# One exponential, one cast and one subtraction of 2048 columns per head in place of two halves

## The chip, the cores and the metric

The kernel runs on one core of one Trainium2 chip. The metric is the device time of one execution, in microseconds. TensorE does the matmuls, ScalarE the activations (ACT in the rows), VectorE the elementwise work (DVE), GpSimd small operations and scattered stores (POOL), and SyncE (SP) issues most transfers.

## What is computed

A decoder layer over x of 4 x 512 tokens of 512 values. Of the three parts only the attention matters here:

```
q = layernorm(x) @ Wq        # 16 heads of 128
k, v = layernorm(x) @ Wkv    # one key and value head, shared by all 16
sim  = (4 * l2norm(q)) @ (4 * l2norm(k)).T
attn = softmax(sim)
out  = layernorm((attn @ v) @ Wout)
x = x + out
```

Then every token goes through one of four gated experts chosen by its id, and then through a feed-forward with weights of three values. All is in fp32 in the reference.

## The kernel before, in words

**Precision.** fp32 products are made of 16-bit ones: a number is split into a high part (a cast) and a low part (the number less its high part), and three matmuls take high x high, high x low and low x high (split_products, lines 252 to 254).

**Heads as steps.** The attention is a loop of 64 steps (STEPS), one per batch and head; step g is head g % 16 of batch g // 16. A step has 512 queries by 512 keys: scores is [keys, queries] in four PSUM banks, S, 2048 columns of fp32 on 128 partitions. ScalarE takes the exponential of S into P32 in SBUF (exponentials). VectorE casts P32 to bf16 (ph) and subtracts (pl), in probabilities. TensorE multiplies both with V (values); the sum of the probabilities is a column of ones beside V. ph and pl are double buffered, P32 and S are not.

**What TensorE does in step g**, in this order: scores(g), values(g - 1), in six steps of the 64 keys_values (the projection for the next batch), from step 16 on outputs(g - 16), a quarter of the output projection of one tile, and up to step 57 queries(g + 6), the query projection of four heads for one tile of 128 tokens. The order is written out by hand in each engine's program, and semaphores tie the engines together.

**The query bank.** queries(u) writes one PSUM bank, QB. ScalarE takes squares (query_squares, line 834), GpSimd a reciprocal root (query_norm), ScalarE writes the high part (query_high, 843) and VectorE the low part (query_low, line 1171), both straight from the bank. For u under 20 the bank alternates between QB and OUTB, and queries(u) waits for query_low(u - 2); from u = 21 all use QB, and queries(u) waits for query_low(u - 1):

```
                elif u >= 20:
                    pe.wait_ge(q_lo, u if u > 20 else 19)
```

**What ScalarE does in step g:** query_squares(g + 5), exponentials of both halves, query_high(g + 5), for some steps a cast of inputs, head_high(g - 1) in two pairs (line 862: the head's result scaled by the reciprocal of its sum), then small pieces of other work: query weights in steps 1 to 4, copies and squares of keys and values, sums and rounding of the feed-forward's weights.

**What VectorE does in step g:** probabilities of half 0, head_sums(g - 1, 0) (a reciprocal, line 1188), query_low(g + 5), head_sums(g - 1, 1), probabilities of half 1, head_low(g - 1) (line 1194), then normalization of inputs and of finished rows, and rounding.

**Semaphores around the change:** s_ps counts halves of scores, p_exp halves of exponentials, p_lo halves of subtractions. scores(g) waits half by half until the exponential of step g - 1 has read S; exponentials(g) wait half by half until the subtraction of step g - 1 has read P32; values(g) waits for both halves of p_lo and for head_low(g - 1), which has read O.

Of the kernel before, what the change touches and what calls it, by code (L numbers as in the profile page):

```python
# [13 lines left out]
ALU = mybir.AluOpType  # L14
ACT = mybir.ActivationFunctionType
# [4 lines left out]
HEADS, DH = 16, 128  # L20
# [3 lines left out]
STEPS = B * HEADS  # L24
# [14 lines left out]
def decoder_layer(nc, x, ids, ctx_w, g_norm, Wq, Wkv, Wout, g_out, w1, w2, out):  # L39
# [8 lines left out]
    with stack:  # L48
# [175 lines left out]
        def ph(g):  # L224
            return P16[:, (g % 2) * 4096:(g % 2) * 4096 + 2048].bitcast(BF16)

        def pl(g):
            return P16[:, (g % 2) * 4096 + 2048:(g % 2) * 4096 + 4096]
# [307 lines left out]
        def _(pe):  # L536
            def keys_values(n):
                b, j = divmod(n, 2)
                bank = kvbank(n)
                for i in range(2):  # L540
                    t = 2 * j + i
                    pe.wait_ge(xt[t], 16 * (b + 1))
                    if n == 0:
                        pe.wait_ge(wkv_lo, 1)
                    if n >= 2 and i == 0:
                        pe.wait_ge(p_exp, 2 * (HEADS * (b - 1) + 11 + j) + 1)
                    for c in range(DC):
                        lh = [XT[b % 2][:, (s * DC + c) * N + t * P:(s * DC + c) * N + (t + 1) * P]
                              for s in range(2)]
                        rh = [WKV[:, (s * DC + c) * 256:(s * DC + c + 1) * 256] for s in range(2)]  # L550
                        last = split_products(bank[:, i * 256:(i + 1) * 256], lh[0], lh[1], rh[0], rh[1],
                                              c == 0, c == DC - 1)
                last.then_inc(kv_ps, 1)
# [19 lines left out]
            def scores(g):  # L573
                b, h = divmod(g, HEADS)
                grp, hh = divmod(g, 4)
                if h == 0:
                    pe.wait_ge(kt, 16 * (b + 1))
                if hh == 0:
                    for t in range(NT):
                        pe.wait_ge(qt[t], 16 * (grp + 1))  # L580
                for half in range(2):
                    if g == 0:
                        pe.wait_ge(q_lo, 4)
                    else:
                        pe.wait_ge(p_exp, 2 * (g - 1) + half + 1)
                    if half == 0 and kv_at(g - 1) is not None:
                        pe.wait_ge(kv_f, kv_at(g - 1) - 1)
                    for j in (2 * half, 2 * half + 1):
                        last = split_products(
                            S[:, j * 512:(j + 1) * 512], KT[:, b % 2, j * P:(j + 1) * P],  # L590
                            KT[:, b % 2, N + j * P:N + (j + 1) * P], QT[grp % 2][:, hh * N:(hh + 1) * N],
                            QT[grp % 2][:, (4 + hh) * N:(5 + hh) * N], True, True)
                    last.then_inc(s_ps, 1)

            def values(g):
                b = g // HEADS
                pe.wait_ge(p_lo, 2 * g + 2)
                if g % HEADS == 0:
                    pe.wait_ge(v_lo, 2 * b + 2)
                if g == 0:  # L600
                    pe.wait_ge(k_lo, 2)
                for t in range(NT):
                    if t % 2 == 0 and g >= 1:
                        pe.wait_ge(o_lo, 2 * (g - 1) + t // 2 + 1)
                    o = o_half(t // 2)[:, t % 2, :]
                    for j in range(NT):
                        a = j * N + t * P
                        nc.tensor.matmul(o, ph(g)[:, a:a + P], V[:, b % 2, j, 0:129], start=j == 0,  # L608
                                         stop=False)
                        nc.tensor.matmul(o[:, 0:128], ph(g)[:, a:a + P], V[:, b % 2, j, 130:258],  # L610
                                         start=False, stop=False)
                        last = nc.tensor.matmul(o, pl(g)[:, a:a + P], V[:, b % 2, j, 0:129], start=False,  # L612
                                                stop=j == NT - 1)
                    if t % 2:
                        last.then_inc(o_ps, 1)

            def outputs(n):
                b, s = divmod(n, HEADS)
                t, q = divmod(s, 4)
                k = b * NT + t  # L620
                if n == 0:
                    pe.wait_ge(q_lo, 20)
                if t == 0 and b == 0:
                    pe.wait_ge(wo_lo, 4 * (q + 1))
                if q == 0:
                    if k == 4:
                        pe.wait_ge(w_set, 1)
                    if 1 <= k <= 12:
                        pe.wait_ge(out_cp, k)
                    elif k > 12:  # L630
                        pe.wait_ge(p_exp, 2 * STEPS)
                for i in range(4):
                    h = 4 * q + i
                    if t == 0:
                        pe.wait_ge(ot[i], (b * 4 + q + 1) * 16)
                        if b == 3:
                            pe.wait_ge(ot_l[i], (q + 1) * 16)
                    lh = [OT[:, ot_block(b, h, s_, t) * P:(ot_block(b, h, s_, t) + 1) * P] for s_ in range(2)]
                    w = h * 2 * D
                    last = split_products(outbank(k), lh[0], lh[1], WOA[:, w:w + D], WOA[:, w + D:w + 2 * D],  # L640
                                          h == 0, h == HEADS - 1)
                last.then_inc(out_c, 1)
# [131 lines left out]
        def _(act):  # L774
# [69 lines left out]
                                                ACT.Copy, scale=rn[:, u % 2, i:i + 1])  # L844
                last.then_inc(q_hi, 1)

            def exponentials(g, half):
                act.wait_ge(s_ps, 2 * g + half + 1)
                if g >= 1:
                    act.wait_ge(p_lo, 2 * (g - 1) + half + 1)  # L850
                nc.scalar.activation(P32[:, half * 1024:(half + 1) * 1024], S[:, half * 1024:(half + 1) * 1024],  # L851
                                     ACT.Exp, bias=off_p).then_inc(p_exp, 1)

            def head_high(g):
                if g >= 2:
# [91 lines left out]
            for g in range(STEPS):  # L947
                b, h = divmod(g, HEADS)
                if out_at(g, 0) is not None:
                    out_copy(out_at(g, 0))  # L950
                if g >= 1 and g + 5 < STEPS:
                    query_squares(g + 5)
                for half in range(2):
                    exponentials(g, half)
                if g >= 1 and g + 5 < STEPS:
                    query_high(g + 5)
                if prep_at(g, 3) is not None:
                    input_high(prep_at(g, 3))
                if out_at(g, 3) is not None:
                    h_high(out_at(g, 3))  # L960
                if g >= 1:
                    head_high(g - 1)
                if kv_at(g) is not None:
                    kv_copy(kv_at(g))
                if kv_at(g) is not None:
                    key_squares(kv_at(g))
                    value_high(kv_at(g))
                if kv_at(g - 1) is not None:
                    key_high(kv_at(g - 1))
                if 1 <= g < 1 + DC:  # L970
                    query_weight(3, g - 1)
                for p in piece_at(g):
                    weight_sum(p)
                if b == 1:
                    ctx_high(h)
                if g >= 2 * HEADS + 3:
                    tern_low(g - 2 * HEADS - 3)
                if g >= 2 * HEADS + 1:
                    tern_scale(g - 2 * HEADS - 1)
# [84 lines left out]
        def _(dve):  # L1064
# [108 lines left out]
                        rn[:, u % 2, i:i + 1], qtok(u)[:, i * P:(i + 1) * P], ALU.mult, ALU.subtract)  # L1173
                last.then_inc(q_lo, 1)

            def probabilities(g, half):
                dve.wait_ge(p_exp, 2 * g + half + 1)
                if g >= 2:
                    dve.wait_ge(o_ps, 2 * (g - 1))
                cols = slice(half * 1024, (half + 1) * 1024)  # L1180
                nc.vector.tensor_copy(ph(g)[:, cols], P32[:, cols]).then_inc(p_hi, 1)  # L1181
                dve.wait_ge(p_hi, 2 * g + half + 1)
                nc.vector.tensor_tensor(pl(g)[:, cols], P32[:, cols], ph(g)[:, cols], ALU.subtract  # L1183
                                        ).then_inc(p_lo, 1)

            def head_sums(g, bank):
                dve.wait_ge(o_ps, 2 * g + bank + 1)
# [117 lines left out]
            for g in range(STEPS):  # L1305
# [2 lines left out]
                    ctx_low(g - 1 - HEADS)  # L1308
                if kv_at(g - 2) is not None:
                    key_low(kv_at(g - 2))  # L1310
                probabilities(g, 0)
                if g == 2 * HEADS:
                    weight_scales_set()
                if g >= 1:
# [2 lines left out]
                    query_low(g + 5)  # L1317
                if g >= 1:
                    head_sums(g - 1, 1)
                probabilities(g, 1)  # L1320
                if g >= 1:
                    head_low(g - 1, 0)
                    head_low(g - 1, 1)
# [325 lines left out]
```

## Time and profile before

| | us |
|---|---|
| median of 3 runs | 966.65 |
| the runs | 963.07, 966.65, 969.02 |
| profiled execution, its own time | 969.39 |
| its span | 967.7 |
| TensorE busy | 920.4 (95%) |
| VectorE busy | 698.8 (72%) |
| ScalarE busy | 616.8 (64%) |
| GpSimd busy | 324.8 (34%) |

The 64 steps fill the span from about 40 to 680 us, the rest is the experts and the feed-forward. Busy shares are means over the span and say nothing of order: an engine with time to spare can still be late where another waits for it. The trace gives each instruction's start and length, and for an idle time ahead of one what ended it. A matmul of 512 columns is shown with 0.38 us, but the next one starts 0.216 us after it, since they are pipelined; so stretches of TensorE are measured from start to start.

### The profile page before, as it was taken

To read this page: it belongs to the slowest core of one execution; us is meant where nothing else is said; L and a number is where in the kernel's file an instruction comes from. 1 tells how busy PE (TensorE), PEld (TensorE's weight loads), DVE (VectorE), ACT (ScalarE), POOL (GpSimd) and SP (SyncE) were. 2 spreads that over 40 slices of the span, in tenths; PEclk is the share of its full clock that TensorE was granted. 3 is DMA by queue.
4 is the path that set the end of the run, shared out by engine and by line. 5 is a ranking of instruction groups with operands and counts; after the bars stand their busy time and mean duration, and the time that the engine had idled before them with its cause. 6 is when DMAs were issued, how large, how long until landed. Compare 5 with 4: busy or idle time off the path is not lost.

```text
span 967.7 us, 19126 instructions
## 1 busy us (share of the span) xinstructions
PE 920.4 (95%) x6577; PEld 520.8 (54%) x6592; DVE 698.8 (72%) x1535; ACT 616.8 (64%) x1571; POOL 324.8 (34%) x450
## 2 busy tenths in 40 slices
PE   5999999999999999999999999999896999999994
PEld 3466676555656566556665565566442444444441
DVE  6799977687786768778677667778262478877782
ACT  4877767667777666667666676665201269988472
POOL 3578866113332323334231322221141012322221
PEclk9999999999999999999999999999997999999999
DMA  9647557567776553564444444349976988544253
GB/s 244 170 89 143 111 109 130 137 165 180 207 169 159 135 127 99 120 143 115 100 99 121 99 115 109 95 120 173 205 183 140 182 191 162 128 99 97 63 131 87
DMA packets 305663, 131.86 MB, mean 136 GB/s; under 512 B 275296, under 2 KB 279904, under 8 KB 305568
## 3 DMA queue, kind: packets, MB, share of 16 engines
q1 hardware_dynamic: 301648, 117.77, 55.3%
q0 software_dynamic: 3920, 12.86, 4.0%
q8 instruction: 54, 0.88, 0.4%
q14 instruction: 41, 0.34, 0.1%
HBM read 42.76 MB, written 20.99 MB: 66 GB/s over the span
## 4 chain that ended last, share of the span: by engine, by line
PE 79%; DVE 5%; issue 3%; ACT 3%; DMA 3%; SPq 2%; POOL 1%; DVEq 0%; ACTq 0%; POOLq 0%
PE S L252 7%; PE S L254 7%; PE S L253 7%; PE O L610 6%; PE O L608 5%; PE QB L252 5%; PE QB L254 5%; PE QB L253 5%; PE O L612 5%; PE OUTB L252 5%; PE OUTB L253 5%; PE OUTB L254 5%; PE S L732 3%; PE OUTB L750 3%; PE O L702 2%
## 5 line engine op out<-in xcount | busy, mean ns | idle before, releaser
L608 PE MATMUL O<-V,P 128*128 128x129 f16 x1024 | 179.0, 219 | 1.3 <-DVE P L1183 1.2
L610 PE MATMUL O<-V,P 128*128 128x128 f16 x1024 | 179.1, 221 | 0.0
L612 PE MATMUL O<-V,P 128*128 128x129 f16 x1024 | 178.9, 218 | 0.0
L1181 DVE CAST P<-P 128x1024 bf16<-128x1024 f32 x128 | 93.9, 733 | 114.8 <-ACT P L851 114.7
L1183 DVE TENSOR_TENSOR P<-P 128x1024 f16<-128x1024 f32 x128 | 160.7, 1255 | 4.4
L851 ACT ACTIVATE P<-S,cst 128x1024 f32<-128x1024 f32 x128 | 142.5, 1116 | 27.2 <-PE S L254 25.4
L1517 POOL TENSOR_SCALAR qst<-qs 128x4 f32<-128x4 f32 x64 | 14.7, 229 | 351.8 <-ACT junk L834 351.8
L834 ACT ACTIVATE junk<-QB 128x128 bf16<-128x128 f32 x208 | 54.8, 278 | 102.8 <-PE QB L254 102.8
L862 ACT ACTIVATE OTOK<-O,rd 128x128 f16<-128x128 f32 x256 | 80.8, 376 | 40.8 <-DVE rd L1188 40.3
L608 PEld LDWEIGHTS O<-V,P 128*128 128x128 bf16 x1024 | 98.5, 96 | 9.5 <-DVE P L1183 2.3
L610 PEld LDWEIGHTS O<-V,P 128*128 128x128 bf16 x1024 | 99.2, 97 | 7.2
L612 PEld LDWEIGHTS O<-V,P 128*128 128x128 f16 x1024 | 100.8, 98 | 0.0
L252 PE MATMUL S<-XQA,KT 128*128 128x512 f16 x256 | 97.2, 380 | 0.3 <-DMA XQA<-P 0.3
L253 PE MATMUL S<-XQA,KT 128*128 128x512 f16 x256 | 97.0, 379 | 0.0
L254 PE MATMUL S<-XQA,KT 128*128 128x512 f16 x256 | 97.0, 379 | 0.0
L252 PE MATMUL OUTB<-WOA,OTA 128*128 128x512 f16 x208 | 79.5, 382 | 2.4 <-ACT OS L873 2.4
L252 PE MATMUL QB<-WQA,XQA 128*128 128x512 f16 x208 | 79.3, 381 | 2.5 <-DVE QTOKR L1171 2.5
L254 PE MATMUL QB<-WQA,XQA 128*128 128x512 f16 x208 | 79.6, 383 | 0.0
L253 PE MATMUL QB<-WQA,XQA 128*128 128x512 f16 x208 | 79.4, 382 | 0.0
L253 PE MATMUL OUTB<-WOA,OTA 128*128 128x512 f16 x208 | 79.4, 382 | 0.0
L254 PE MATMUL OUTB<-WOA,OTA 128*128 128x512 f16 x208 | 79.3, 381 | 0.0
L1518 POOL TENSOR_TENSOR rn<-qst,half 128x4 f32<-128x4 f32 x64 | 71.8, 1123 | 5.4
(238 smaller groups left out, 1952.2 us busy)
## 6 DMA issues: line engine op xcount, KB each, us to landing
SIDE<-in_L_ffn_w_dram SPq DMA_DIRECT2D x64, 256.0 KB, 3.2
OTA<-sorted_rows SPq DMA_DIRECT2D x4, 1028.0 KB, 6.5
OTA<-in_L_attn_Wq_dram SPq DMA_DIRECT2D x4, 1024.0 KB, 7.5
SIDE<-in_L_attn_Wout_dram SPq DMA_DIRECT2D x16, 256.0 KB, 3.1
SIDE<-in_ctx_dram SPq DMA_DIRECT2D x16, 256.0 KB
ctx_split<-SIDE SPq DMA_DIRECT2D x16, 256.0 KB, 3.7
ROWB<-in_x_dram SPq DMA_DIRECT2D x16, 256.0 KB, 3.3
w_tern<-SIDE SPq DMA_DIRECT2D x32, 128.0 KB, 3.0
```

Of the source, the lines that this page charges most:

```text
L252: nc.tensor.matmul(o, lh, rh, start=first, stop=False)
L253: nc.tensor.matmul(o, lh, rl, start=False, stop=False)
L254: return nc.tensor.matmul(o, ll, rh, start=False, stop=last)
L608: nc.tensor.matmul(o, ph(g)[:, a:a + P], V[:, b % 2, j, 0:129], start=j == 0, stop=False)
L610: nc.tensor.matmul(o[:, 0:128], ph(g)[:, a:a + P], V[:, b % 2, j, 130:258], start=False, stop=False)
L612: last = nc.tensor.matmul(o, pl(g)[:, a:a + P], V[:, b % 2, j, 0:129], start=False, stop=j == NT - 1)
L834: last = nc.scalar.activation(junk[:, i * P:(i + 1) * P], qbank(u)[:, i * P:(i + 1) * P], ACT.Square, scale=16.0 / WS, accum_out=qs[:, u % ...
L851: nc.scalar.activation(P32[:, half * 1024:(half + 1) * 1024], S[:, half * 1024:(half + 1) * 1024], ACT.Exp, bias=off_p).then_inc(p_exp, 1)
L862: last = nc.scalar.activation(OTOK[:, g % 2, t * P:(t + 1) * P], o_tile(t), ACT.Copy, scale=rd[:, g % 2, t:t + 1])
L1181: nc.vector.tensor_copy(ph(g)[:, cols], P32[:, cols]).then_inc(p_hi, 1)
L1183: nc.vector.tensor_tensor(pl(g)[:, cols], P32[:, cols], ph(g)[:, cols], ALU.subtract).then_inc(p_lo, 1)
L1518: nc.gpsimd.tensor_tensor(rn[:, s, :], qst[:, s, :], half4[:, :], ALU.pow).then_inc(q_rn, 1)
```

## The change

The exponential, the cast and the subtraction of a step each become one instruction over 2048 columns. p_exp and p_lo count steps rather than halves, and all waits on them are recounted. scores(g) waits for the whole exponential of step g - 1 before either half.

```diff
@@ scores and values, TensorE
-                        pe.wait_ge(p_exp, 2 * (g - 1) + half + 1)
+                        pe.wait_ge(p_exp, g)
...
-                pe.wait_ge(p_lo, 2 * g + 2)
+                pe.wait_ge(p_lo, g + 1)
@@ ScalarE
-            def exponentials(g, half):
-                act.wait_ge(s_ps, 2 * g + half + 1)
+            def exponentials(g):
+                act.wait_ge(s_ps, 2 * g + 2)
                 if g >= 1:
-                    act.wait_ge(p_lo, 2 * (g - 1) + half + 1)
-                nc.scalar.activation(P32[:, half * 1024:(half + 1) * 1024], S[:, half * 1024:(half + 1) * 1024],
-                                     ACT.Exp, bias=off_p).then_inc(p_exp, 1)
+                    act.wait_ge(p_lo, g)
+                nc.scalar.activation(P32[:, :], S[:, :], ACT.Exp, bias=off_p).then_inc(p_exp, 1)
@@ VectorE
-            def probabilities(g, half):
-                dve.wait_ge(p_exp, 2 * g + half + 1)
+            def probabilities(g):
+                dve.wait_ge(p_exp, g + 1)
                 if g >= 2:
                     dve.wait_ge(o_ps, 2 * (g - 1))
-                cols = slice(half * 1024, (half + 1) * 1024)
-                nc.vector.tensor_copy(ph(g)[:, cols], P32[:, cols]).then_inc(p_hi, 1)
-                dve.wait_ge(p_hi, 2 * g + half + 1)
-                nc.vector.tensor_tensor(pl(g)[:, cols], P32[:, cols], ph(g)[:, cols], ALU.subtract
-                                        ).then_inc(p_lo, 1)
+                nc.vector.tensor_copy(ph(g), P32[:, :]).then_inc(p_hi, 1)
+                dve.wait_ge(p_hi, g + 1)
+                nc.vector.tensor_tensor(pl(g), P32[:, :], ph(g), ALU.subtract).then_inc(p_lo, 1)
@@ the loop over steps, VectorE
-                probabilities(g, 0)
+                probabilities(g)
                 if g == 2 * HEADS:
                     weight_scales_set()
                 if g >= 1:
@@
                     query_low(g + 5)
                 if g >= 1:
                     head_sums(g - 1, 1)
-                probabilities(g, 1)
```

On VectorE the work of a step after step 32 stands in this order before. CAST and the TENSOR_TENSOR behind it are probabilities, RECIPROCAL is head_sums, QTOKR is written by query_low, OTOK by head_low:

```order
L1181 CAST P<-P 128x1024 [waits o_ps,p_exp]
L1183 TENSOR_TENSOR P<-P 128x1024 [waits p_hi]
L1188 RECIPROCAL rd<-O 128x2 [waits o_ps]
L1171 SCALAR_TENSOR_TENSOR QTOKR<-QB,rn,QTOKR 128x128 [waits q_hi]
L1171 SCALAR_TENSOR_TENSOR QTOKR<-QB,rn,QTOKR 128x128 x3
L1188 RECIPROCAL rd<-O 128x2 [waits o_ps]
L1181 CAST P<-P 128x1024 [waits o_ps,p_exp]
L1183 TENSOR_TENSOR P<-P 128x1024 [waits p_hi]
L1194 SCALAR_TENSOR_TENSOR OTOK<-O,rd,OTOK 128x128 [waits o_hi]
```

The same place in the changed kernel:

```order
L1178 CAST P<-P 128x2048 [waits o_ps,p_exp]
L1180 TENSOR_TENSOR P<-P 128x2048 [waits p_hi]
L1184 RECIPROCAL rd<-O 128x2 [waits o_ps]
L1169 SCALAR_TENSOR_TENSOR QTOKR<-QB,rn,QTOKR 128x128 [waits q_hi]
L1169 SCALAR_TENSOR_TENSOR QTOKR<-QB,rn,QTOKR 128x128 x3
L1184 RECIPROCAL rd<-O 128x2 [waits o_ps]
L1190 SCALAR_TENSOR_TENSOR OTOK<-O,rd,OTOK 128x128 [waits o_hi]
```

The second half's cast and subtraction have moved ahead of both reciprocals and of query_low; head_low follows the second reciprocal at once.

On ScalarE, in a step of the first batch, before (junk is written by query_squares, P from S by exponentials, QTOKR by query_high, OTOK by head_high):

```order
L834 ACTIVATE junk,qs<-OUTB 128x128 [waits q_rn,q_sq,q_ps]
L834 ACTIVATE junk,qs<-OUTB 128x128 x3
L851 ACTIVATE P<-S,cst 128x1024 [waits p_lo,s_ps] x2
L843 ACTIVATE QTOKR<-OUTB,rn 128x128 [waits qt3,q_rn]
L843 ACTIVATE QTOKR<-OUTB,rn 128x128 x3
L862 ACTIVATE OTOK<-O,rd 128x128 [waits o_rd,ot1]
```

and changed:

```order
L834 ACTIVATE junk,qs<-OUTB 128x128 [waits q_rn,q_sq,q_ps]
L834 ACTIVATE junk,qs<-OUTB 128x128 x3
L851 ACTIVATE P<-S,cst 128x2048 [waits p_lo,s_ps]
L843 ACTIVATE QTOKR<-OUTB,rn 128x128 [waits qt3,q_rn]
L843 ACTIVATE QTOKR<-OUTB,rn 128x128 x3
L861 ACTIVATE OTOK<-O,rd 128x128 [waits o_rd,ot1]
```

Nothing has changed place here; the two exponentials are one, and it waits for both halves of the scores. head_high still waits for o_rd, the reciprocals on VectorE, and the next step's query_squares stand behind it. TensorE's order is the same as before.

## Rows read from the trace of the kernel before

**Rows 1.** Windows: stretch, length, busy us of each engine, granted clock, DMA share, GB/s.

```profile
176.00:620.00 444.00, 444.00 (x3556) 267.77 (x3555) 326.65 (x765) 305.94 (x920) 129.13 (x162) 1.00 0.55 133
```

**Rows 2.** Timeline, TensorE, one step: start us, length us, line, instruction, tiles.

```profile
401.57 0.38 PE L252 MATMUL S<-XQA,KT 128*128 128x512 f16 x1
...
406.91 0.38 PE L252 MATMUL OUTB<-WOA,OTA 128*128 128x512 f16 x1
...
409.50 0.38 PE L252 MATMUL QB<-WQA,XQA 128*128 128x512 f16 x1
...
412.09 0.38 PE L252 MATMUL S<-XQA,KT 128*128 128x512 f16 x1
```

**Rows 3.** Timeline, TensorE, the scores' start in two early steps.

```profile
54.66 0.38 PE L252 MATMUL S<-XQA,KT 128*128 128x512 f16 x1
...
62.59 0.38 PE L252 MATMUL S<-XQA,KT 128*128 128x512 f16 x1
```

**Rows 4.** Timeline, ScalarE, the step of rows 2; in brackets idle time before.

```profile
403.07 1.12 ACT L851 ACTIVATE P<-S,cst 128x1024 f32<-128x1024 f32 x1 [0.15 <-PE S L254]
404.36 1.12 ACT L851 ACTIVATE P<-S,cst 128x1024 f32<-128x1024 f32 x1 [0.18 <-PE S L254]
```

**Rows 5.** Timeline, VectorE, the same step.

```profile
404.21 0.69 DVE L1181 CAST P<-P 128x1024 bf16<-128x1024 f32 x1 [2.52 <-ACT P L851]
404.94 1.23 DVE L1183 TENSOR_TENSOR P<-P 128x1024 f16<-128x1024 f32 x1
...
406.54 1.13 DVE L1171 SCALAR_TENSOR_TENSOR QTOKR<-QB,rn,QTOKR 128x128 f16<-128x128 f32 x4 [0.29 <-ACT QTOKR L843]
```

**Rows 6.** Timeline, ScalarE, steps 15 and 16.

```profile
165.43 0.26 ACT L834 ACTIVATE junk<-QB 128x128 bf16<-128x128 f32 x1
...
166.43 2.13 ACT L851 ACTIVATE P<-S,cst 128x1024 f32<-128x1024 f32 x2
...
171.04 0.63 ACT L862 ACTIVATE OTOK<-O,rd 128x128 f16<-128x128 f32 x2 [0.41 <-DVE rd L1188]
171.56 0.63 ACT L884 ACTIVATE SIDE<-SIDE 128x512 f32<-128x512 f32 x1
...
176.78 1.11 ACT L851 ACTIVATE P<-S,cst 128x1024 f32<-128x1024 f32 x1 [0.28 <-PE S L254]
```

**Rows 7.** Timeline, VectorE, step 15.

```profile
168.32 1.51 DVE L1183 TENSOR_TENSOR P<-P 128x1024 f16<-128x1024 f32 x1
```

**Rows 8.** Timeline, TensorE, after two of its idle times.

```profile
170.99 0.39 PE L252 MATMUL QB<-WQA,XQA 128*128 128x512 f16 x1 [2.54 <-DVE QTOKR L1171]
...
949.04 3.19 PE L750 MATMUL OUTB<-WOA,KT 128*128 128x512 bf16 x13 [1.72 <-DMA KT<-XHLR]
```

**Rows 9.** Groups by line and shape; the last two of 60 to 160 us.

```profile
L1025 ACT ACTIVATE WOA<-S,fs 128x512 f32<-128x512 f32 x2 | 1.3, 684 | 0.0
L1237 DVE CAST HR<-OS 128x512 f16<-128x512 f32 x4 | 1.7, 427 | 0.1
L1146 DVE TENSOR_TENSOR XHLR<-XSR,XHLR 128x512 f16<-128x512 f32 x12 | 8.2, 680 | 0.0
L779 ACT ACTIVATE WQA<-OTA,gws 128x512 f16<-128x512 f32 x12 | 8.0, 720 | 0.7 <-DMA OTA<-in_L_attn_Wq_dram 0.7
...
L1183 DVE TENSOR_TENSOR P<-P 128x1024 f16<-128x1024 f32 x24 | 33.0, 1374 | 0.8
L1181 DVE CAST P<-P 128x1024 bf16<-128x1024 f32 x24 | 19.9, 827 | 8.0 <-ACT P L851 8.0
```

**Rows 10.** Timeline, ScalarE: the second exponentials of steps 1, 58 and 63.

```profile
49.35 1.12 ACT L851 ACTIVATE P<-S,cst 128x1024 f32<-128x1024 f32 x1 [0.75 <-DVE P L1183]
...
630.52 1.11 ACT L851 ACTIVATE P<-S,cst 128x1024 f32<-128x1024 f32 x1 [0.18 <-PE S L254]
...
670.16 1.12 ACT L851 ACTIVATE P<-S,cst 128x1024 f32<-128x1024 f32 x1 [0.18 <-PE S L254]
```

**Rows 11.** Windows, columns as in rows 1, behind the first idle time of rows 8.

```profile
173.00:174.00 1.00, 1.00 (x4) 0.43 (x3) 1.00 (x4) 0.00 (x0) 0.00 (x0) 0.50 0.16 32
```

More of the change, by code:

```diff
@@ L545, in keys_values @@
                     if n >= 2 and i == 0:
-                        pe.wait_ge(p_exp, 2 * (HEADS * (b - 1) + 11 + j) + 1)
+                        pe.wait_ge(p_exp, HEADS * (b - 1) + 11 + j + 1)
                     for c in range(DC):
@@ L630, in outputs @@
                     elif k > 12:
-                        pe.wait_ge(p_exp, 2 * STEPS)
+                        pe.wait_ge(p_exp, STEPS)
                 for i in range(4):
@@ L952, in _ @@
                     query_squares(g + 5)
-                for half in range(2):
-                    exponentials(g, half)
+                exponentials(g)
                 if g >= 1 and g + 5 < STEPS:
```

## The prediction

> **What bounds the kernel now.** I read the windows first, then TensorE's timeline over one head, then what ScalarE and VectorE do beside it, then every idle gap of TensorE. From 176 to 620 us TensorE is busy for all 444.00 us at full clock, while VectorE and ScalarE have about 26% and 31% to spare [rows 1]. One head there takes TensorE 412.09 - 401.57 = 10.52 us: scores, values of the head before, 2.59 us of outputs, and from 7.93 us (409.50) the queries for six heads on, 2.59 us [rows 2]. Heads 1 to 15 have no outputs and take 62.59 - 54.66 = 7.93 us [rows 3]. So TensorE is the bound, and the change, which touches ScalarE and VectorE alone, can gain hardly anything on it. The question is whether the cover of their chain still holds.
>
> That chain has two ends in TensorE. VectorE must finish the probabilities before the values, one head later, and it must finish query_low, which frees the only query bank QB, before the next queries start. The second is the tight one. Today query_low stands between the halves: VectorE is done with half 0 at 406.17, starts query_low at 406.54 and ends it at 407.66 [rows 5], against the queries at 409.50 [rows 2]: 1.84 us of slack. The change puts all 2048 columns ahead of query_low.
>
> **The change, part by part.** Call T the start of a head's scores on TensorE and E the end of its exponential.
>
> *Exponential.* It now needs both halves of the scores; the second half's started at T + 2.79 (404.36) [rows 2, 4]. Its length: 1.12 us for 1024 columns [rows 4], and an activation from PSUM to fp32 of 512 took 0.684 [rows 9], so 0.43 to 0.44 per 512 more, 1.12 + 0.86 = 1.98; I take 1.97. Two halves back to back took 2.13 [rows 6], the upper bound. E = T + 4.76.
>
> *Cast and subtraction.* The cast started 0.02 after the exponential's end, the subtraction 0.04 after the cast's [rows 4, 5]. A cast of 512 took 0.427 against 0.69 for 1024: 1.23 for 2048. A subtraction of 512 took 0.680 against 1.23: 2.31 for 2048 [rows 5, 9]. So both are done at E + 0.02 + 1.23 + 0.04 + 2.31 = E + 3.60. The upper bound is the halves' durations added, 2 x (0.69 + 1.23) = 3.84; a lower one than 3.5 has no row for it, since both operations grow with their columns.
>
> *query_low, then the queries.* Head 15 shows what follows a late subtraction: that ended at 168.32 + 1.51 = 169.83, and the queries started at 170.99, held by VectorE's QTOKR: 1.16 later [rows 7, 8]. So the queries start at T + 4.76 + 3.60 + 1.16 = T + 9.52 where today they start at T + 7.93. Nothing else covers this: they stand in TensorE's order ahead of the next scores. **A loss of 1.59 us per head, period 12.11.** It does not wash out: the next exponential waits for the next scores, these for the queries, these for query_low, so the ring closes on itself.
>
> *How many heads.* A single bank is waited on from query 21, that is from head 15, up to head 57. Heads 27, 28, 43 and 44 have keys_values on TensorE too, 24 matmuls of 256 columns, so the 2.59 us that 12 of 512 take [rows 2]; that fills the gap, and they last 13.1 us before and after. Heads 16 to 57 are 42, less 4 is 38: 38 x 1.59 = **+60.4**.
>
> *Heads 0 to 15.* There the queries wait for the query_low of the head before and are not held, but another ring appears. reciprocals, query_low and head_high now come after the whole subtraction, and ScalarE computes the squares for the next head only after both pairs of head_high. From head 15: subtraction's end 169.83, second pair of head_high from 171.04 to 171.56 (+1.73); four squares take 166.43 - 165.43 = 1.00; then the exponential, 1.97 [rows 6, 7]. Ring: 3.60 + 1.73 + 1.00 + 1.97 = 8.30. In that stretch cast and subtraction are slower, 827 and 1374 ns for a half against 690 and 1230 [rows 9] (GpSimd scales the output weights beside them): 2 x (0.137 + 0.144) = +0.56, so 8.86 against 7.93. Fourteen steps from head 1 to head 15: 14 x 8.86 = 124.0, plus on ScalarE, inside the ring, four query weights at 0.62 net of 0.72 [rows 9] (2.5), key and value work of heads 11 to 13 (about 3.9: a copy of 512 columns, two squares and the values' cast for each of two pairs, and a pair of key casts, by the nearest rows), two weight sums of 512 (1.3): 131.7. Before: end of exponential 1 at 49.35 + 1.12 = 50.47, of 15 at 168.56: 118.1 [rows 6, 10]. **+13.6**, and +0.6 from the start (head 0's exponential is whole, its cast waits for query weights either way).
>
> *Head 15 to 16.* Before, the second exponential of head 16 ended at 176.78 + 1.29 + 1.12 = 179.19 [rows 4, 6], 10.63 after that of 15. Now 12.11, +0.5 for slow VectorE, and 1.7 for TensorE's clock (it idled 2.54 us before, and longer now: next paragraph): 14.3, **+3.7**.
>
> *The clock.* After the gap of 2.54 us the granted clock fell to 0.50, the lower of the two levels (1.2 GHz against 2.4), with the second from 173 to 174 us wholly at it [rows 11]. Cost: at full clock the first exponential of head 16 would have started at 170.99 + 2.59 + 1.50 = 175.08 (1.50 is 403.07 - 401.57) and it started at 176.78 [rows 2, 4, 6]: 1.70 us. The new gaps are 9.52 - 7.93 - 0.17 (the last matmul's tail) = 1.42 us in the profile's count. A gap of 1.72 us late in the kernel was followed by 13 matmuls in 3.19 us, full clock [rows 8]. So I take no fall for the 38.
>
> *Heads 58 to 63.* No queries. Ring: 3.60, head_high pairs at once (1.2), two ternary operations on ScalarE (1.2), 1.97: 8.0, with one output copy 8.5, five steps, 40.6; before 670.16 - 630.52 = 39.64 [rows 10]. **+1.0.** The end of the probabilities is 3.6 after the last exponential in both; from there on nothing is changed.
>
> *What goes later at no cost.* head_low of the head before now ends about 1.5 us after query_low, near T + 11; the values that wait for it start 2.59 us into the next head, at T + 14.7. The transposes of heads are read 16 heads later. Those of queries are issued after query_low, some 2 us later in a head, and are needed two heads on.
>
> **Sum:** 0.6 + 13.6 + 3.7 + 60.4 + 1.0 = +79.3 on the profiled execution's 969.4, 1048.7. The median of the runs is 2.7 lower: **1047 us** (rounded up from 1046).
>
> **The rivals.**
>
> *A. The clock falls in the new gaps.* Each of the 38 would cost the 1.70 of head 15: +64.6, 1111 us. For it: gaps recur every 12 us, and what decides lies somewhere between gaps of 1.72 and 2.54 us [rows 8], so that a head with a slow cast gets close. Against: 1.42 is below a gap that cost nothing, and TensorE is busy 88% of the time. The Trainium skill, page "TensorE: Matmul & The Clock Gate", section "A second HAM failure mode: psum-queue depth-cycling", tells of small idles between groups of matmuls, repeated often enough that the clock goes up and down; that would be this case. No stretch of this trace shows such a pattern, so it neither agrees nor disagrees; by that rule the time would be the 1111 us. Chance 0.12 for most gaps, with some in between.
>
> *B. Only the single-bank wait counts.* If the ring of heads 0 to 15 closes faster than by my sum (ScalarE's parts overlap more, VectorE is not slowed), TensorE's slack takes most of it: +3 there in place of +13.6: 1036. Chance 0.13.
>
> *C. Not slower.* It needs query_low to end before T + 7.93, so the wide cast and subtraction in 2.0 us rather than 3.6. That would be so if most of an operation's time were fixed, since two are saved on VectorE and one on ScalarE. Then TensorE stays the bound and the time is that of before, 966, perhaps 1 less since the gap of head 15 shrinks; the point of turning is a pair under 2.0 us. The rows speak against it: from 512 to 1024 columns the subtraction grows by 0.55 of 1.23 us [rows 9]. The Trainium skill, page "Perfetto Trace Analysis", section "Optimizing Scalar/DVE Operations", says that grouping into larger operations can raise throughput where the engine is saturated. By the throughput alone it saves about 0.2 us of VectorE a head, and VectorE is not the bound from 176 us on. Chance 0.03.
>
> **Range and chances.** Forecast 0.72, B 0.13, A 0.12, C 0.03. Within the forecast: a period of 12.0 to 12.5 (exponential 1.96 to 2.13, pair 3.5 to 3.84) is 56 to 75, and heads 0 to 16 give between 12 and 22, so 1036 to 1064. B's own low end is 6 below its 1036; at the high end a third of the gaps losing clock is +21 on 1064. The range is 1030 to 1085. A change of 1% (10 us) is what a measurement of this kernel can tell: faster by more 0.01, within 0.03, slower 0.96.
>
> **What would show it.** TensorE in heads 16 to 57: a period near 12.1 us, a gap near 1.4 us ahead of the QB matmuls with VectorE's QTOKR as releaser, about 38 of them, 54 us in all. The exponential at 1.97, cast 1.23, subtraction 2.31. ScalarE's exponentials of heads 5 to 10 spaced 8.9 us. Clock at 1.00 from 200 us to 700. I am wrong if the gap ahead of QB is missing, if the clock shows falls in that stretch, or if the exponentials of the first heads stand 7.9 us apart.

## The result: 8.4% slower, 1046.5 us

The changed kernel takes 1046.49 us (median of 4 runs, 1045.26 to 1047.79) against 967.39 us for the kernel before on the same chip: a ratio of 1.084, 95% interval 1.082 to 1.087. The forecast was 1047. Its profiled execution took 1046.07 us with a span of 1044.3 us, 76.6 more than before.

The page of the changed kernel, first engine line and three groups (line, engine, operation, tiles, shapes, count | busy us, mean ns | idle before, released by):

```profile
PE 928.9 (89%) x6592; PEld 515.9 (49%) x6592; DVE 678.5 (65%) x1407; ACT 598.7 (57%) x1507; POOL 307.4 (29%) x450
...
L1178 DVE CAST P<-P 128x2048 bf16<-128x2048 f32 x64 | 79.1, 1235 | 216.4 <-ACT P L851 193.7
...
L851 ACT ACTIVATE P<-S,cst 128x2048 f32<-128x2048 f32 x64 | 126.4, 1974 | 64.9 <-PE S L254 62.5
L1180 DVE TENSOR_TENSOR P<-P 128x2048 f16<-128x2048 f32 x64 | 148.4, 2319 | 2.2
```

VectorE and ScalarE each do about 20 us less work than before (698.8 and 616.8) and the kernel is 79 us slower. By busy time the change is a saving; what it costs is order. The three operations last what the rows of shorter ones gave: 1.97, 1.23 and 2.31 us were forecast.

The waits of TensorE, longest in total first (waiting line, released by: us, times, longest):

```profile
PE QB L252 <- DVE QTOKR L1169: 58.7, 38, 6.0
PE OUTB L647 <- DVE P L1144: 11.6, 1, 11.6
PE QB L652 <- DMA sorted_h<-HR,posu: 9.5, 1, 9.5
PE O L608 <- DVE OTOK L1190: 9.4, 13, 2.5
PE OUTB L252 <- DVE wsc L1261: 3.2, 1, 3.2
```

The second and third were there before (10.9 and 9.5 us), the fourth and fifth are new. The first is the gap ahead of QB: 5.95 us of it in head 15, where the kernel before waited 2.54, and 52.8 us in 37 of the heads from 16 to 57. Head 32 isn't among them, since its wait stands in the fifth line.

One head on TensorE (answers rows 2), then ScalarE (rows 4) and VectorE (rows 5) in it:

```profile
436.57 0.38 PE L252 MATMUL S<-XQA,KT 128*128 128x512 f16 x1
...
441.91 0.38 PE L252 MATMUL OUTB<-WOA,OTA 128*128 128x512 f16 x1
...
446.07 0.39 PE L252 MATMUL QB<-WQA,XQA 128*128 128x512 f16 x1 [1.42 <-DVE QTOKR L1169]
...
448.68 0.38 PE L252 MATMUL S<-XQA,KT 128*128 128x512 f16 x1
```

```profile
439.36 1.97 ACT L851 ACTIVATE P<-S,cst 128x2048 f32<-128x2048 f32 x1 [1.45 <-PE S L254]
```

```profile
441.36 1.23 DVE L1178 CAST P<-P 128x2048 bf16<-128x2048 f32 x1 [3.74 <-ACT P L851]
442.62 2.29 DVE L1180 TENSOR_TENSOR P<-P 128x2048 f16<-128x2048 f32 x1
444.83 0.16 DVE L1184 RECIPROCAL rd<-O 128x2 f32<-128x2 f32 x1
444.91 1.11 DVE L1169 SCALAR_TENSOR_TENSOR QTOKR<-QB,rn,QTOKR 128x128 f16<-128x128 f32 x4
```

With T = 436.57: exponential at T + 2.79, its end T + 4.76, subtraction's end T + 8.34, queries T + 9.50 (forecast 2.79, 4.76, 8.36, 9.52), next head T + 12.11. These operations form a ring: scores, exponential, cast, subtraction, first reciprocal, query_low, queries, next scores. Each starts as soon as the one before it allows, so nothing in the ring has slack, though every engine idles: ScalarE 1.45 us before its exponential, VectorE 3.74 before its cast, TensorE 1.42 before the queries. The mean granted clock rounds to 1.00 from 197 to 708 us; inside that stretch it fell once, for 3.4 us in head 32 (below):

```profile
197.00:708.00 511.00, 455.20 (x3569) 266.64 (x3570) 321.94 (x699) 299.22 (x888) 99.44 (x164) 1.00 0.47 115
```

### The profile page after: what moved, and what is told of

The parts are those of the page before. It is cut to its first block, busy times and chain, and to the rows that moved or that the text cites. A ratio compares the mean times of both kernels' runs of the same rounds, so it can differ in the third digit from the quotient of the medians.

```text
span 1044.3 us, 18824 instructions
## 1 busy us (share of the span) xinstructions
PE 928.9 (89%) x6592; PEld 515.9 (49%) x6592; DVE 678.5 (65%) x1407; ACT 598.7 (57%) x1507; POOL 307.4 (29%) x450
## 4 chain that ended last, share of the span: by engine, by line
PE 42%; DVE 32%; ACT 14%; issue 5%; DMA 2%; POOL 1%; SPq 0%; DVEq 0%; ACTq 0%; POOLq 0%
DVE P L1180 13%; ACT P L851 9%; DVE P L1178 7%; DVE QTOKR L1169 5%; PE S L254 5%; PE S L252 5%; PE S L253 5%; PE QB L252 5%; PE QB L253 4%; PE QB L254 4%; PE S L732 3%; PE OUTB L750 3%; PE O L702 2%; ACT junk L834 1%; PE O L705 1%
## 5 line engine op out<-in xcount | busy, mean ns | idle before, releaser
L1178 DVE CAST P<-P 128x2048 bf16<-128x2048 f32 x64 | 79.1, 1235 | 216.4 <-ACT P L851 193.7
L851 ACT ACTIVATE P<-S,cst 128x2048 f32<-128x2048 f32 x64 | 126.4, 1974 | 64.9 <-PE S L254 62.5
L1180 DVE TENSOR_TENSOR P<-P 128x2048 f16<-128x2048 f32 x64 | 148.4, 2319 | 2.2
L1190 DVE SCALAR_TENSOR_TENSOR OTOK<-O,rd,OTOK 128x128 f16<-128x128 f32 x256 | 76.3, 342 | 14.2 <-ACT OTOK L861 14.1
L254 PE MATMUL OUTB<-WOA,OTA 128*128 128x512 f16 x208 | 79.3, 381 | 0.0
```

Source lines behind the costliest of these rows:

```text
L254: return nc.tensor.matmul(o, ll, rh, start=False, stop=last)
L851: nc.scalar.activation(P32[:, :], S[:, :], ACT.Exp, bias=off_p).then_inc(p_exp, 1)
L1178: nc.vector.tensor_copy(ph(g), P32[:, :]).then_inc(p_hi, 1)
L1180: nc.vector.tensor_tensor(pl(g), P32[:, :], ph(g), ALU.subtract).then_inc(p_lo, 1)
L1190: last = nc.vector.scalar_tensor_tensor(OTOK[:, g % 2, 512 + t * P:512 + (t + 1) * P], o_tile(t), rd[:, g % 2, t:t + 1], OTOK[:, g % 2, t ...
```

## The sum, term by term

| | forecast | measured |
|---|---|---|
| start to exponential 1 | +0.6 | +0.8 |
| heads 1 to 15 | +13.6 | +9.6 |
| head 15 to 16 | +3.7 | +3.8 |
| heads 16 to 58 | +60.4 | +64.1 |
| heads 58 to 63 | +1.0 | +1.6 |
| from there to the end | 0 | -3.3 |
| span | +79.3 | +76.6 |

Measured values are distances between ends of exponentials: 516.56 against 452.45 us from head 16 to 58, 127.75 against 118.10 from 1 to 15. Three terms were off by 3 to 4 us each, one up and two down. That the total still fits within 3 us is partly luck.

**The scales of head 32 were overlooked: +3.5.** One head in the middle takes 15.65 us rather than 12.11. On VectorE, there:

```profile
389.39 1.23 DVE L1178 CAST P<-P 128x2048 bf16<-128x2048 f32 x1 [4.78 <-ACT P L851]
390.65 2.29 DVE L1180 TENSOR_TENSOR P<-P 128x2048 f16<-128x2048 f32 x1
392.87 0.15 DVE L1258 TENSOR_SCALAR wsc<-OUTB 128x2 f32<-128x2 f32 x1
393.05 0.17 DVE L1260 TENSOR_SCALAR wsc<-wsc 128x2 f32<-128x2 f32 x1
393.25 0.17 DVE L1261 RECIPROCAL wsc<-wsc 128x2 f32<-128x2 f32 x1
```

weight_scales_set reads two columns out of OUTB, and the outputs of that step overwrite OUTB. It stood behind half a subtraction and stands behind a whole one. TensorE idled 3.24 us in place of the 1.42 ahead of QB, and the granted clock was at its lower level behind it, which is the rest of the 3.5 us:

```profile
394.00:396.00 2.00, 2.00 (x6) 0.64 (x5) 1.81 (x8) 0.83 (x3) 0.00 (x0) 0.50 0.14 32
```

The line stands in the diff's context, between probabilities and head_sums. The prediction asked what query_low is late for and did not ask it of that line.

**Heads 1 to 15: 4 us less than forecast.** The ring is the one named (shown below), but the slow casts and subtractions of this stretch did not double with the width, as the sum had assumed. From 60 to 175 us:

```profile
L1180 DVE TENSOR_TENSOR P<-P 128x2048 f16<-128x2048 f32 x13 | 31.2, 2402 | 0.5
L851 ACT ACTIVATE P<-S,cst 128x2048 f32<-128x2048 f32 x13 | 25.9, 1995 | 1.2 <-PE S L254 1.2
L1178 DVE CAST P<-P 128x2048 bf16<-128x2048 f32 x13 | 16.0, 1227 | 23.7 <-ACT P L851 22.8 <-PE O L612 0.9
```

The cast takes 1227 ns, the same as alone, where the halves had 827 for 690 [rows 9]. The subtraction takes 0.11 us more than its 2292 later on. Together that is 0.11 a head in place of the 0.56 that the sum took, 6.3 us less over 14 heads. The term was 4.0 us too large, so its other parts together were some 2.3 us too small; which of them is not shown.

This does not say that a wide cast is immune to GpSimd. It met other work there. Before (VectorE, GpSimd at the same time):

```profile
84.86 1.17 DVE L1181 CAST P<-P 128x1024 bf16<-128x1024 f32 x1
84.34 1.16 POOL L1525 TENSOR_TENSOR WOA<-SIDE,WOA 128x512 f16<-128x512 f32 x1
```

and changed:

```profile
105.15 1.23 DVE L1178 CAST P<-P 128x2048 bf16<-128x2048 f32 x1 [1.82 <-ACT P L851]
104.64 2.19 POOL L1518 TENSOR_SCALAR SIDE<-SIDE 128x512 f32<-128x512 f32 x1
```

From 60 to 175 us 12 of the 27 half casts took 0.80 to 1.17 us, and each of the 12 overlapped GpSimd's cast or its TENSOR_TENSOR into WOA. The others took 0.67 to 0.70, all but one of them beside GpSimd's scaling (the TENSOR_SCALAR) or its small operations; the one met GpSimd's cast and was not slowed. None of the 13 wide casts overlapped the two that write WOA.

Five of the 13 wide subtractions took 2.58 us rather than 2.29, which is 0.29 more, and a slow half took mostly 1.51 for 1.22, again 0.29: a subtraction of twice the width lost no more. Heads 5 to 10 come 8.31 us apart where the subtraction took 2.29 and 8.60 where it took 2.58, which fits the 8.30 of the ring without GpSimd. GpSimd's own scaling took 2.15 to 2.54 us in twelve of its thirteen times in this stretch and 1.49 in one, where before it took anything from 1.49 to 2.33.

**From the last exponential to the end: 3.3 us less, mostly not by the change.** In the profiled execution of the kernel before, ScalarE waited 4.41 us for the load of a feed-forward weight, so the copy that frees OUTB came late, TensorE idled 2.42 us, and the clock fell:

```profile
679.59 0.81 ACT L901 ACTIVATE SIDE<-SIDE,cst,wsc 128x512 f32<-128x512 f32 x1 [4.41 <-DMA SIDE<-in_L_ffn_w_dram]
680.30 0.58 ACT L873 ACTIVATE OS<-OUTB 128x512 f32<-128x512 f32 x1
```

The kernel before with one query in another bank (under "A better version of either kernel") has the same order there. It has no such wait, and takes 291.7 us from the last exponential to the end against 296.4, while the change takes 293.1. So the -3.3 is mostly owed to that wait in one execution of the kernel before. The medians, 79.1 us apart, do not rest on one execution. In the change TensorE idles 2.50 us ahead of the last values, which wait for head_low of head 62, and the clock stays at 1.00.

## Experiments

Each was compared with the kernel before on the same chip. Since the chips differ by up to 0.5%, ratios count: before is 1, the change 1.084. Spacings of exponentials from the profile carry the verdicts; from head 1 to head 63 the kernel before takes 620.8 us and the change 700.0.

### Which of the wide operations costs: the exponential alone

```diff
 exponentials(g)                  # one of 2048 columns, as changed
-probabilities(g)
+probabilities(g, 0)
 ...                              # head_sums, query_low, head_sums
+probabilities(g, 1)
```

> The exponential is one of 2048 columns as in the change, but VectorE's cast and subtraction are two halves in their old places around the reciprocals and query_low. Theory (query_low comes late behind the wide subtraction): the exponential ends at T + 4.76, half 0 is subtracted 1.9 us later, query_low ends near T + 7.85, just ahead of the queries at T + 7.93. So heads 16 to 57 stay at 10.52 us, no gap ahead of QB beyond that of head 15, 965 to 973 us. Rival (what costs is that scores wait for the whole exponential, and the exponential for both halves of the scores): the time is near the change's, 1035 to 1050.

974.29 us, ratio 1.010 (1.006 to 1.014): just past the range of the theory, far from the rival. From head 1 to 63 it takes 627.6 us. The heads from 16 to 57 are within 0.1 us of their old spacing but for two. TensorE's waits from 196 to 640 us:

```profile
PE OUTB L252 <- DVE wsc L1263: 1.6, 1, 1.6
PE QB L252 <- DVE QTOKR L1169: 0.9, 1, 0.9
```

So the whole exponential, and scores that wait for all of it, are nearly free; the slack of 0.07 us ahead of the queries held in 37 of 38 heads. The scales of head 32 show up again at half the delay, since they stand behind half a subtraction. What is lost between heads 1 and 63, 6.8 us, lies mostly in the first 16 heads (3.7) and in these two places.

### Cast and subtraction alone

```diff
 exponentials(g, 0); exponentials(g, 1)   # halves, as before
-probabilities(g, 0)
+probabilities(g)                         # waits for both
 ...
-probabilities(g, 1)
```

> The exponential stays in two halves; cast and subtraction are wide, ahead of query_low, as in the change. Theory: the second exponential ends at T + 3.91, the subtraction 3.60 later, the queries start 1.16 after it at T + 8.67 against 7.93: 0.74 us in each of 38 heads, 28 us, period 11.26; in heads 1 to 15 ScalarE's ring is as in the change or 0.15 longer, +10; with heads 15 to 16 and 32 (3 to 7 us), 1005 to 1018. Rival (the whole exponential is the cost): 965 to 975.

1016.10 us, ratio 1.053 (1.049 to 1.058), in the range. The period is 11.25 (forecast 11.26), the gap 0.56 us:

```profile
443.25 0.39 PE L252 MATMUL QB<-WQA,XQA 128*128 128x512 f16 x1 [0.56 <-DVE QTOKR L1171]
```

That is 0.73 a head, and the whole exponential on top makes it 1.59. The exponential costs next to nothing alone and 0.86 us a head together with the other two: the end of one half of 1024 columns is 0.85 us ahead of the end of one operation of 2048, and with the slack used up by VectorE each such delay counts in full. The costs of the parts do not add up here: 1.0% and 5.3% make 8.4%.

### query_low ahead of the wide operations

```diff
+if g == 2 * HEADS: weight_scales_set()
+head_sums(g - 1, 0); query_low(g + 5); head_sums(g - 1, 1)
 probabilities(g)
-if g == 2 * HEADS: weight_scales_set()
-head_sums(g - 1, 0); query_low(g + 5); head_sums(g - 1, 1)
```

> The change with all its wide operations, but on VectorE the two reciprocals, query_low and the scales of step 32 stand ahead of the cast and the subtraction. Theory: query_low waits for query_high, 1.06 us after the exponential, and ends near T + 7.0, ahead of the queries; heads 16 to 57 at 10.52 us with no gap; the subtraction ends near T + 10.5, in time for the values at T + 13.1. In the first 15 heads head_low now ends some 0.6 to 0.9 us after the values would start, 5 to 10 us in all. 965 to 978. Rival (wide operations cost by themselves, by their length or by what they hold up): above 1020.

974.34 us, ratio 1.011 (1.007 to 1.015). All operations are as wide as in the change; 7 of its 8 per cent are gone by order alone (the scales of head 32, 3.5 us, are among what was moved). From 197 to 637 us TensorE never idles:

```profile
197.00:637.00 440.00, 440.00 (x3512) 264.60 (x3510) 316.50 (x683) 290.30 (x871) 103.10 (x162) 1.00 0.58 132
```

This shows the main term: the period is 10.52 us again, with the same wide operations. Most of what remains is in the first heads (125.5 us from 1 to 15 against 118.1), where head_low is late for the values by up to 1.73 us (7.4 us of TensorE's waits, in 7 of them).

### The ring of the first heads: a cure that made another wait

```diff
+if 1 <= g < HEADS: head_sums(g - 1, 0); head_sums(g - 1, 1)
 probabilities(g)
```

> The change, but in heads 1 to 15 alone both reciprocals stand ahead of the cast, so that head_high no longer waits for the subtraction; query_low stays behind it. Theory (in those heads the ring runs subtraction, reciprocals, second head_high, squares, exponential): exponentials of heads 5 to 10 come every 7.9 to 8.2 us in place of 8.3 to 8.9, 5 to 9 us less up to head 15, the rest as in the change: 1036 to 1043. Rival (the first heads are slow because VectorE works against GpSimd there): no difference, 1045 to 1048.

1051.07 us, ratio 1.090 (1.086 to 1.094): outside both ranges. That it is slower than the change is not shown, since the intervals overlap, and 4.8 of the 7.3 us by which its profiled execution is longer lie ahead of the end of exponential 1, where the edit changes nothing. What is shown is that nothing was gained: heads 1 to 15 take 128.5 us, in the change 127.8. The exponentials of heads 5 to 10 stand 8.4 to 9.5 us apart, in the change 8.3 to 8.6. VectorE's waits from 55 to 170 us have a new first place:

```profile
DVE rd L1184 <- PE O L612: 24.3, 21, 3.4
```

The reciprocals read the sums that the values of the head before leave in PSUM, and TensorE is not done with them when the exponential ends. Ahead of the cast they hold VectorE up by 24.3 us. The ring through head_high was cut (ScalarE's waits for the reciprocals from 55 to 175 us fell from 42.4 to 3.8 us), and one through TensorE put in its place. So the experiment can't tell the theory from the rival; its expectation missed what queues behind a waiting instruction.

### The same cure without a new wait

```diff
 probabilities(g)
 head_sums(g - 1, 0)
+if g < HEADS: head_sums(g - 1, 1)
 query_low(g + 5)
-head_sums(g - 1, 1)
+if g >= HEADS: head_sums(g - 1, 1)
```

> The change, but in heads 1 to 15 the second reciprocal stands right behind the first, both still behind the subtraction, and query_low behind them. Nothing waits for anything new. Theory (the ring of the first heads is subtraction, second reciprocal, second head_high, squares, exponential): head_high's second pair starts 1.1 us earlier, the ring drops from 8.3 to 7.3 us, so TensorE's 7.93 sets the pace, or head_low where GpSimd slows VectorE: exponentials every 7.9 to 8.3 us, 4 to 7 us less up to head 15, 1040 to 1043. If the ring is another one (values that wait for head_low): no difference, 1045 to 1048.

1041.29 us, ratio 1.081 (1.077 to 1.086), inside the theory's range; its interval overlaps that of the change, so the spacing decides: heads 1 to 15 take 121.0 us in place of 127.8, those of heads 5 to 10 are 7.8 to 8.1 us apart. An operation of 0.16 us moved past one of 1.11 gives 6.8 us. The edit also lets head_low end a little earlier, so by itself it doesn't exclude the other ring, of values that wait for head_low. The trace of the change does: from 55 to 175 us its exponentials waited for scores only twice, 1.2 us in all, and ScalarE waited 42.4 us for the reciprocals. The ring of subtraction, second reciprocal, second head_high, squares and exponential is what set the pace.

### The scales of head 32

```diff
+if g == 2 * HEADS: weight_scales_set()
 probabilities(g)
-if g == 2 * HEADS: weight_scales_set()
```

> The change, but in step 32 alone the scales of the ternary weights are set ahead of the cast. Theory (outputs of that step wait for them, and they come behind the wide subtraction): the 3.24 us gap ahead of OUTB near 393 us goes, head 32 to 33 takes 12.1 us in place of 15.65, 1043 us. If the scales wait for something else, no change.

1044.92 us, ratio 1.083 (1.078 to 1.088), two runs. The head takes 12.1 us, the gap ahead of OUTB is gone. 3.5 us is too small for the comparison of times and plain in the trace.

### Rival A: the same gap, made longer

```diff
 nc.vector.tensor_copy(ph(g), P32[:, :])
+if HEADS <= g < STEPS - AHEAD:
+    link(nc.vector.tensor_tensor(pl(g)[:, 0:n], P32[:, 0:n], ph(g)[:, 0:n], ALU.subtract))
 nc.vector.tensor_tensor(pl(g), P32[:, :], ph(g), ALU.subtract)
```

n = 256, 512 and 1024, two runs of each; link makes the next operation wait for this one.

> The change with 256 columns of the subtraction computed twice in heads 16 to 57, 0.41 + 0.04 us: gaps of 1.87 us, period 12.56, so 1046 + 17 = 1063 without falls of the clock. Gaps of 1.42 and 1.53 lost no clock and gaps of 2.14 in every second head; with falls in a fourth of the heads 1079.

> The change with the first 512 columns of the subtraction computed once more ahead of it in heads 16 to 57, 0.68 + 0.04 us on VectorE. Theory of the sum: each of the 38 gaps ahead of QB grows by 0.72 to 2.14 us and the period to 12.83, so 1046 + 27 = 1074 (kv heads stay covered). If the clock falls after gaps of 2.1 us, up to 1.7 us more for each: up to 1138, and the granted clock shows 0.5 in a third of the stretch.

> The same with 1024 columns, 1.23 + 0.04 us: gaps of 2.69 us, longer than the 2.54 us after which the clock fell in the kernel before. Period 13.38 at full clock, so 1046 + 48 = 1094, plus 1 or 2 in each of the four heads with keys and values. With a fall after every gap 1.7 us more each: 1159. I expect falls in most, 1130 to 1160.

| | gap, us | heads with a fall, of 37 | period without, with | us, ratio |
|---|---|---|---|---|
| the change | 1.42 (1.53) | 0 | 12.11, - | 1046.49, 1.084 |
| n = 256 | 1.88 (1.97) | 2 | 12.57, 14.33 | 1067.37, 1.107 |
| n = 512 | 2.14 (2.23) | 19 | 12.83, 14.52 | 1108.17, 1.149 |
| n = 1024 | 2.67 (2.76) | 8 | 13.37, 14.77 | 1110.19, 1.151 |

(In brackets the few longer gaps, most of them beside heads with keys and values, where the period without a fall is 0.07 us longer. The 37 are heads 16 to 57 without the four with keys and values and without head 32, which waits at OUTB; a fall is counted where the granted clock went to 0.50.) Two windows with n = 512, in neighbouring heads:

```profile
448.00:451.00 3.00, 3.00 (x16) 1.35 (x15) 0.77 (x2) 1.14 (x8) 0.68 (x2) 1.00 0.88 178
460.00:463.00 3.00, 3.00 (x9) 1.06 (x7) 2.65 (x7) 1.41 (x3) 0.00 (x0) 0.51 0.84 175
```

The first is at the upper level, with 16 matmuls in 3 us, the second at the lower, with 9. A fall costs 1.69 us of the head, the 1.70 that the prediction read from head 15 of the kernel before. In the change none of the 37 gaps cost clock, so rival A is out at 1.42 us. With 0.45 us more on VectorE 2 of the 37 heads lost clock, with 0.72 more 19, about half: what the rival describes begins there. For n = 512 half of the heads, 19 x 1.69 = 32 us, paid it.

The last row was forecast wrong. The longest gaps lost clock less often, 8 times rather than in most heads, and the time is nearly the same. So the length of the gap alone does not decide: with n = 512 every second head falls, with n = 1024 every fifth or sixth. What else does, these runs do not show.

### A better version of either kernel

Two tries. The kernel before, with the query of head 15 in the other bank:

```diff
-OUTB[:, :] if u % 2 and u < 20 else QB[:, :]
+OUTB[:, :] if u % 2 and u < 22 else QB[:, :]
```

with the waits of queries(21), queries(22) and of the first outputs recounted.

> The kernel before, with halves, but query 21 goes to the bank OUTB rather than QB, and the first outputs wait for query_low of 21. Theory: the gap of 2.54 us in head 15 and the fall of the clock after it (1.7 us) go; in their place the outputs of head 16 wait some 0.7 us for query_low. 963 to 966 us, 0.2 to 0.4% under the kernel before. Rival: the gap only moves to the outputs, no difference.

963.46 us against 964.01 over 12 and 16 runs, ratio 0.998 (0.996 to 1.000). From head 14 to head 17 it is 27.5 us in place of 30.8; the one gap left there is

```profile
180.48 0.39 PE L252 MATMUL OUTB<-WOA,OTA 128*128 128x512 f16 x1 [0.99 <-DVE QTOKR L1171]
```

The trace shows the 3.2 us, the times can't tell 0.3% from nothing with certainty. And the wide operations with both orders mended:

```diff
+if g >= HEADS:                     # scales, head_sums, query_low, head_sums
 probabilities(g)
+if g < HEADS:                      # head_sums, head_sums, query_low
```

> All wide operations of the change, with the order mended in both stretches: up to head 15 both reciprocals and then query_low behind the subtraction, from head 16 reciprocals, query_low and scales ahead of the cast; and query 21 in bank OUTB. Heads 16 to 57 at 10.52, first heads at 7.93 to 8.3 (+0 to +5 against before), the gap of head 15 and its clock gone (-3), a gap of about 1.5 us at the outputs of head 16. Level with the kernel before within 0.5%: 961 to 970.

972.29 us, ratio 1.010 (1.006 to 1.014), a little above the range. Heads 16 to 57 are at 10.52, but heads 1 to 15 take 121.0 us and the outputs of head 16 wait 2.93 us, with the clock down after it. That wait was put at 1.5. ScalarE shows where the rest comes from:

```profile
175.20 1.14 ACT L861 ACTIVATE OTOK<-O,rd 128x128 f16<-128x128 f32 x4 [2.73 <-DVE rd L1184]
...
178.44 2.01 ACT L851 ACTIVATE P<-S,cst 128x2048 f32<-128x2048 f32 x1
```

The scores of head 16 start at 173.19, so its exponential could start at T + 2.79. It starts at T + 5.25, since head 15 still has the order of the first heads: head_high waits there for the subtraction, and the squares and the exponential of head 16 stand behind it. query_low(21), for which the outputs wait, is late by that much; 0.9 us of it TensorE had already spent waiting ahead of the values. Even where TensorE never waits for them (heads 17 to 57), the wide operations bring nothing, since it is TensorE that is full. Halves are the better form here.

## Why the prediction was right

- **TensorE is the bound, a gain is not to be had.** Right: with every wait for the wide operations removed from head 16 on, that stretch is as long as before (query_low ahead of the wide operations).
- **The queries wait for query_low, 1.59 us in 38 heads.** Right: a period of 12.11 us, to the hundredth, by the single bank QB. There are 37 such waits, not 38: in head 32 TensorE waits at OUTB instead. (The 38 waits of the list above have head 15 among them.) The price came from three growths by columns, and from one place in the trace of before, head 15, where the wait already existed once and which showed the delay from the end of a subtraction to the first matmul.
- **Heads 1 to 15.** The mechanism was right, shown by the second reciprocal; its size was 4 us too large, 9.6 for 13.6, and heads 5 to 10 stand 8.3 to 8.6 us apart where 8.9 was named as the sign. The step that was mis-sized is the 0.56 for VectorE slowed beside GpSimd: it took the mean loss of a half twice, and measured 0.11. That is 6.3 us; the other parts together were put 2.3 us too low and hide part of it.
- **Head 15 to 16, with its clock:** 3.8 for 3.7, by luck. The 0.5 for a slow VectorE did not come, and the clock cost 2.35 us rather than 1.70 (exponential 16 started at 191.47; at full clock, 2.59 + 2.79 us behind the queries' start at 183.75, it would have been 189.12). The gap is 5.95 us rather than 2.54, and the clock was low for 6.8 us rather than 3.4. In the four other runs with the change's order up to there, the same gap cost 1.62 to 2.71 us of clock.
- **Heads with keys and values** stay at 13.14.
- **The clock holds in gaps of 1.42 us.** Right, for 37 of 37 gaps. The one fall from 200 to 700 us is that of head 32, which the prediction had not seen coming. The Trainium skill, page "TensorE: Matmul & The Clock Gate", section "A second HAM failure mode: psum-queue depth-cycling", tells of small idles repeated so often that the clock goes up and down. That describes the runs with longer gaps (19 heads of 37 at 2.14 us), not this kernel.
- **Missed:** the scales of head 32 (+3.5). They nearly cancel the 4.0 us too many of heads 1 to 15, so that the medians are 79.1 us apart where the sum had 79.3 is luck to that extent. The main term, 60.4 of it, is not.
- **Rival B** (the first heads take +3) falls: they took +9.6. **Rival C** (not slower) falls with the durations: cast and subtraction take 3.5 us together, 2.0 was needed. VectorE does save 0.3 us of work a head, and nothing comes of it.

## What to carry to other kernels

Where several engines run an order written by hand, price a wider operation by what stands behind it in its queue: write down, for each instruction that it moves back, who waits for it and with how much slack. Here the slack was 1.84 us and the delay 3.4, on an engine that is idle a quarter of the time. Look in the trace of before for a place where the wait to come already exists once: it gives the price of the step that no duration shows. And read the context lines of the diff, since what stands between the moved pieces moves too.

## What the runs showed of the hardware

- Gaps of TensorE of 1.42 to 1.88 us, one in every 12 to 13 us, lost no clock (37 in the change, 33 with n = 256). The first falls came at 1.96 us (2 of 4 such gaps). At 2.14 us every second head had one, at 2.67 us one in five. Each fall in these heads cost 1.4 to 1.7 us.
- The same gap does not always cost clock. The 2.50 us ahead of the last values stand in seven runs at the same place in the order; the clock fell in two of them (n = 256 and 512) and stayed up in five.
- A half cast on VectorE took 0.80 to 1.17 us for 0.69 only while GpSimd was in its cast or its TENSOR_TENSOR into WOA. Beside GpSimd's TENSOR_SCALAR, halves and wide casts (1227 ns in all 13) took what they take later on, and the TENSOR_SCALAR itself took up to 2.54 us where it has 1.49 at best. Slow subtractions lost the same 0.29 us at 1024 and at 2048 columns.
